# A four-block transformer stack on one core: one of its transposes per tile by VectorE and POOL, and two small products with a PSUM bank per half of the heads

## What is computed

```python
x = x + _L0_attn_ref(_layernorm(x), ...)   # linear attention, 16 heads: phi = silu + 1
x = x + _L0_ffn_ref(_layernorm(x), ...)    # silu(w1 h) * (w2 h), gelu(h1 .), gelu(h2 .), w3
x = x + _L1_attn_ref(_layernorm(x), ...)   # softmax attention over the tile's 512 tokens
x = x + _L1_ffn_ref(_layernorm(x), ...)    # tanh(h @ weight @ aux1 @ aux2 + bias)
```

## Time and profile before

| | us |
|---|---|
| median of 3 runs | 1982.96 |
| lowest and highest | 1981.56, 1984.99 |
| span of the profiled execution | 1981.5 |
| TensorE busy | 1961.9 (99%) |
| VectorE busy | 1289.0 (65%) |
| ScalarE busy | 1020.0 (51%) |
| POOL busy | 406.8 (21%) |

### The profile page before, as it was taken

How to read it: one execution, slowest core, us unless ns; L and a number is a source line. 1 busy time by engine, 2 the same in 40 slices (tenths; PEclk the granted TensorE clock), 3 DMA queues, 4 the chain that set the end, 5 groups by cost and what they waited for, 6 DMA issues and landing times.

```text
span 1981.5 us, 37810 instructions
## 1 busy us (share of the span) xinstructions
PE 1961.9 (99%) x15288; PEld 1895.6 (96%) x15288; DVE 1289.0 (65%) x3292; ACT 1020.0 (51%) x1786; POOL 406.8 (21%) x344
## 2 busy tenths in 40 slices
PE   8999999999999999999999999999999999999998
PEld 7999999999999999999999999999999999999996
DVE  6546768566685665767667676666856667676357
ACT  3445545555554655455554455555546454554433
POOL 1112212212122021311213121121220213112121
PEclk9999999999999999999999999999999999999999
DMA  9600000000000000000000000000000000000000
GB/s 359 224 3 1 22 1 12 11 2 22 1 22 1 1 22 1 22 1 1 22 1 22 1 1 22 1 22 1 23 1 1 22 1 12 1 1 12 1 1 23
DMA packets 24538, 46.03 MB, mean 23 GB/s; under 512 B 1264, under 2 KB 21488, under 8 KB 24176
## 3 DMA queue, kind: packets, MB, share of 16 engines
q1 hardware_dynamic: 24352, 43.41, 6.1%
HBM read 35.02 MB, written 19.92 MB: 28 GB/s over the span
## 4 chain that ended last, share of the span: by engine, by line
PE 97%; DMA 1%; DVE 1%; SPq 1%; issue 0%; ACT 0%; POOL 0%; DVEq 0%; ACTq 0%
PE ffn_fill L1117 49%; PE att_fill L1048 25%; PE ffn_fill L1048 13%; PE ffn_fill L1174 6%; PE att_fill L1136 1%; PE att_fill L1252 1%; DMA scratch_w2T<-in_w2T 1%; DMA w<-scratch_w1T 0%; SPq L543 0%; PE ffn_fill L1285 0%; DVE late_sm L869 0%; PE ffn_fill L1280 0%; ACT late_kv_b L1009 0%; DVE st L671 0%; DVE late_prob_t_lo L864 0%
## 5 line engine op out<-in xcount | busy, mean ns | idle before, releaser
L1117 PE MATMUL ffn_fill<-act_hi,h 128*128 128x256 f32 x4096 | 987.2, 283 | 0.8 <-issue 0.2
L1117 PE MATMUL ffn_fill<-act_lo,h 128*128 128x256 f32 x4096 | 978.2, 280 | 1.2 <-issue 1.2
L1117 PEld LDWEIGHTS ffn_fill<-act_hi,h 128*128 128x128 f32 x4096 | 770.3, 188 | 9.2 <-POOL act_lo L649 3.9
L1117 PEld LDWEIGHTS ffn_fill<-act_lo,h 128*128 128x128 f32 x4096 | 773.1, 189 | 3.6
L976 ACT ACTIVATE whole<-ffn_fill,scales 128x256 f32<-128x256 f32 x512 | 214.0, 469 | 291.3 <-PE ffn_fill L1117 290.1
L649 POOL TENSOR_TENSOR act_lo<-whole,act_hi 128x512 fp32r<-128x512 f32 x128 | 166.8, 1303 | 492.4 <-DVE act_hi L798 492.4
L802 DVE TENSOR_TENSOR act_lo<-whole,act_hi 128x512 fp32r<-128x512 f32 x256 | 183.4, 716 | 112.0 <-ACT act_hi L980 109.7
L1048 PE MATMUL ffn_fill<-half_hi,w 128*128 128x256 f32 x1024 | 245.9, 283 | 0.0
L1048 PE MATMUL ffn_fill<-half_lo,w 128*128 128x256 f32 x1024 | 244.3, 281 | 0.0
L1048 PEld LDWEIGHTS ffn_fill<-half_lo,w 128*128 128x128 f32 x1024 | 193.3, 189 | 0.1
L1048 PEld LDWEIGHTS ffn_fill<-half_hi,w 128*128 128x128 f32 x1024 | 192.5, 188 | 0.4 <-issue 0.2
(11 more groups left out here) (239 smaller groups left out, 3277.8 us busy)
## 6 DMA issues: line engine op xcount, KB each, us to landing
x<-in_L_attn_x SPq DMA_DIRECT2D x16, 512.0 KB, 3.3
out<-x SPq DMA_DIRECT2D x15, 512.0 KB, 2.9
h<-scratch_h1T SPq DMA_DIRECT2D x2, 2048.0 KB, 13.1
h<-scratch_h2T SPq DMA_DIRECT2D x2, 2048.0 KB, 13.4
w<-scratch_w1T SPq DMA_DIRECT2D x1, 1024.0 KB, 7.8
w<-scratch_w2T SPq DMA_DIRECT2D x1, 1024.0 KB, 9.8
w<-scratch_w3T SPq DMA_DIRECT2D x1, 1024.0 KB, 8.3
rows<-in_rows SPq DMA_DIRECT2D x1, 640.0 KB, 5.5
```

The source lines that it names most:

```text
L1117: last = pe.matmul(two(bank)[:, o, :], view(w), view(moving[:, k, :]), start=k == 0 and o == 0 and half == 0, stop=k == KH - 1 and half == ...
```

## The change

In the middle passes c:LT ahead of c:CF becomes c:T: the turn by VectorE into `turned`, the high part by ScalarE, the low part by POOL. On VectorE its two halves stand behind U0 and behind U1, on ScalarE and on POOL the step stands behind U1. AS and AM fill one bank for each half of the heads, which takes two banks more in place of the two that c:LT had. In the start, CHECK1 stands behind a:AQ in the list for that reason. `FIRST` and `END` keep their LT.

```diff
-    "AS": {"att_fill": 1},
-    "AM": {"att_fill": 1, "m_hi_ready": 1},
+    "AS": {"att_fill": 2},
+    "AM": {"att_fill": 2, "m_hi_ready": 2},
...
-    H0 c:CO1 c:CP2 H1 c:CO2 BST1 c:CP3 BNO1 a:AST H2 c:CO3 c:DST H3 NT1 NTL1 c:DNO W0 c:LT a:ANO U0 U1 c:CF a:T
+    H0 c:CO1 c:CP2 H1 c:CO2 BST1 c:CP3 BNO1 a:AST H2 c:CO3 c:DST H3 NT1 NTL1 c:DNO W0 c:T a:ANO U0 U1 c:CF a:T
...
@@ VectorE's order of a middle pass
-    c:LT U2 U3 a:ANO c:CF a:Ta a:Tb G0 G1 a:AKV0 a:AKV1 G2 a:AKV2 a:AKV3 a:AS G3 a:AQ a:AM a:AO n:BST0 H0
+    c:Tb U2 U3 a:ANO c:CF a:Ta a:Tb G0 G1 a:AKV0 a:AKV1 G2 a:AKV2 a:AKV3 a:AS G3 a:AQ a:AM a:AO n:BST0 H0
...
@@ TensorE
                 elif kind == "AS":
                     pe.wait_ge(s["phik_ready"], c.value("phik_ready"))
-                    bank, done = to_fill(pe, c, "att_fill", 0)
                     for g in range(KD):
+                        bank, done = to_fill(pe, c, "att_fill", g)
                         cols_g = slice(g * P, (g + 1) * P)
-                        last = product(four(bank)[:, g, :],
-                                       [(kv_b[:, b, cols_g], xn[:, b, cols_g]) for b in range(NB)])
-                    last.then_inc(done, 1)
+                        product(bank[:, 0:P], [(kv_b[:, b, cols_g], xn[:, b, cols_g]) for b in range(NB)]).then_inc(done, 1)
                 elif kind == "AM":
-                    wait_taken(pe, c, "att_fill", c.ago("att_fill", "AS", 0))
-                    bank, done = to_fill(pe, c, "att_fill", 0)
                     for g in range(KD):
-                        last = product(two(bank)[:, g, :], [(kv[:, g, :], wo[:, g, :])])
-                    last.then_inc(done, 1)
+                        wait_taken(pe, c, "att_fill", c.ago("att_fill", "AS", 0) + g)
+                        bank, done = to_fill(pe, c, "att_fill", g)
+                        product(bank[:, 0:D], [(kv[:, g, :], wo[:, g, :])]).then_inc(done, 1)
...
@@ ScalarE
                 elif kind == "AM":
-                    bank, _ = filled(act, c, "att_fill", 0)
-                    act.activation(m_sb[0], two(bank), ACT.Copy).then_inc(s["m_hi_ready"], 1)
+                    for g in range(KD):
+                        bank, _ = filled(act, c, "att_fill", g)
+                        act.activation(m_sb[0][:, g, :], bank[:, 0:D], ACT.Copy).then_inc(s["m_hi_ready"], 1)
```

More of the change, by code:

```diff
@@ L227 @@
     f:TA0 p:AO a:ANO a:LT LOOK00 LOOK01 f:TA1 m:BST0 a:AKV0 a:AKV1 f:TA2 m:BNO0 m:BT0 CHECK0
-    U0 U1 U2 U3 LOOK10 a:AB LOOK11 a:AKV2 LOOK12 a:AKV3 LOOK13 CHECK1 a:AS a:AQ
+    U0 U1 U2 U3 LOOK10 a:AB LOOK11 a:AKV2 LOOK12 a:AKV3 LOOK13 a:AS a:AQ CHECK1
     G0 a:AM G1 a:AO WIDE G2 LOOK20 LOOK21 FOLD0 TAKE0 G3 LOOK22 LOOK23 CHECK2 LOOK30
@@ L250 @@
     U0 U1 U2 U3 G0 G1a c:LT G1b c:CV c:CZ G2a c:CS0 G2b G3a c:CP0 c:CS1 c:CS2 G3b c:CO0 c:CP1 c:CS3 H0a
-    c:CO1 c:CP2 H0b c:CO2 c:CP3 H1 c:CO3 H2 H3 W0 U0 c:LT U1 U2 U3 c:CFa G0a c:CFb G0b G1 G2 G3 a:AKV0
+    c:CO1 c:CP2 H0b c:CO2 c:CP3 H1 c:CO3 H2 H3 W0 U0 U1 U2 U3 c:CFa G0a c:CFb G0b G1 G2 G3 a:AKV0
     a:AKV1 a:AKV2 a:AKV3 H0a a:AS a:AQ a:AM H0b H1a a:AO H1b H2 H3 W1"""),
@@ L267 @@
     c:CSTa U0 U1 U2 U3 c:CSTb c:CNO c:LT c:CQ c:CV c:CZ c:CS0 G0 c:CP0 c:CS1 c:CS2 c:CO0 G1 c:CP1 c:CS3 G2
-    G3 c:CO1 c:CP2 c:CO2 BST1 c:CP3 H0 BNO1 a:AST c:CO3 c:DSTa H1 c:DSTb NT1a H2 NT1b H3 NTL1 c:DNO W0 U0 U1
-    c:LT U2 U3 a:ANO c:CF a:Ta a:Tb G0 G1 a:AKV0 a:AKV1 G2 a:AKV2 a:AKV3 a:AS G3 a:AQ a:AM a:AO n:BST0 H0
+    G3 c:CO1 c:CP2 c:CO2 BST1 c:CP3 H0 BNO1 a:AST c:CO3 c:DSTa H1 c:DSTb NT1a H2 NT1b H3 NTL1 c:DNO W0 U0 c:Ta U1
+    c:Tb U2 U3 a:ANO c:CF a:Ta a:Tb G0 G1 a:AKV0 a:AKV1 G2 a:AKV2 a:AKV3 a:AS G3 a:AQ a:AM a:AO n:BST0 H0
     n:BNO0 H1 n:NT0a H2 n:NT0b H3 n:NTL0 W1"""),
@@ L284 @@
     U0 U1 U2 U3 c:LT G0 G1 c:CV c:CZ c:CS0 c:CP0 G2 c:CS1 c:CS2 c:CP1 G3 c:CS3 c:CP2 H0 c:CP3 H1 H2 H3 NT1
-    U0 U1 c:LT U2 U3 c:CF G0 a:T G1 G2 a:AKV0 a:AKV1 a:AKV2 a:AKV3 G3 a:AQ a:AM H0 H1 H2 H3 n:NT0"""),
+    U0 U1 c:T U2 U3 c:CF G0 a:T G1 G2 a:AKV0 a:AKV1 a:AKV2 a:AKV3 G3 a:AQ a:AM H0 H1 H2 H3 n:NT0"""),
     "END": order_from("""
@@ L294 @@
     "BODY": order_from("""
-    U0 U1 U2 U3 c:CST c:CB BST1 a:AST c:DST U0 U1 U2 U3 c:CF a:T a:AB n:BST0"""),
+    U0 U1 U2 U3 c:CST c:CB BST1 a:AST c:DST U0 U1 c:T U2 U3 c:CF a:T a:AB n:BST0"""),
     "END": order_from("""
@@ L834, in part @@
                         dve.wait_ge(consts, 7)
-                    bank, out = filled(dve, c, "att_fill", 0)
-                    dve.tensor_tensor(kv[:], four(bank)[:, 0:2, :], head_mask[:, None, :].broadcast_to([P, 2, P]),
-                                      ALU.mult).then_inc(out, 1)
+                    for g in range(KD):
+                        bank, out = filled(dve, c, "att_fill", g)
+                        dve.tensor_tensor(kv[:, g, :], bank[:, 0:P], head_mask[:], ALU.mult).then_inc(out, 1)
                 elif kind == "AM":
-                    bank, out = filled(dve, c, "att_fill", 0)
-                    dve.wait_ge(s["m_hi_ready"], c.value("m_hi_ready", 1))
-                    dve.tensor_tensor(m_sb[1], two(bank), m_sb[0].bitcast(F32), ALU.subtract).then_inc(out, 1)
+                    for g in range(KD):
+                        bank, out = filled(dve, c, "att_fill", g)
+                        dve.wait_ge(s["m_hi_ready"], c.value("m_hi_ready", g + 1))
+                        dve.tensor_tensor(m_sb[1][:, g, :], bank[:, 0:D], m_sb[0][:, g, :].bitcast(F32), ALU.subtract).then_inc(out, 1)
                 elif kind == "CZ":
@@ L1201, in part @@
                     pe.wait_ge(s["phik_ready"], c.value("phik_ready"))
-                    bank, done = to_fill(pe, c, "att_fill", 0)
                     for g in range(KD):
+                        bank, done = to_fill(pe, c, "att_fill", g)
                         cols_g = slice(g * P, (g + 1) * P)
-                        last = product(four(bank)[:, g, :],
-                                       [(kv_b[:, b, cols_g], xn[:, b, cols_g]) for b in range(NB)])
-                    last.then_inc(done, 1)
+                        product(bank[:, 0:P], [(kv_b[:, b, cols_g], xn[:, b, cols_g]) for b in range(NB)]).then_inc(done, 1)
                 elif kind == "AM":
-                    wait_taken(pe, c, "att_fill", c.ago("att_fill", "AS", 0))
-                    bank, done = to_fill(pe, c, "att_fill", 0)
                     for g in range(KD):
-                        last = product(two(bank)[:, g, :], [(kv[:, g, :], wo[:, g, :])])
-                    last.then_inc(done, 1)
+                        wait_taken(pe, c, "att_fill", c.ago("att_fill", "AS", 0) + g)
+                        bank, done = to_fill(pe, c, "att_fill", g)
+                        product(bank[:, 0:D], [(kv[:, g, :], wo[:, g, :])]).then_inc(done, 1)
                 elif kind == "AO":
-                    wait_taken(pe, c, "att_fill", c.ago("att_fill", "AM", 0))
+                    for g in range(KD):
+                        wait_taken(pe, c, "att_fill", c.ago("att_fill", "AM", 0) + g)
                     pe.wait_ge(s["phiq_ready"], c.value("phiq_ready"))
```

## The result

| | before | after |
|---|---|---|
| median of 4 runs | 1983.97 us | 2107.64 us |
| lowest and highest | 1981.56, 1986.16 | 2106.59, 2112.4 |
| span of the profiled execution | 1981.5 us | 2105.9 us |
| ratio, 95% interval | | 1.0634 (1.0618 to 1.0651) |

A forecast was written before the change was run, and what follows sets the result against it. TensorE, busy in 99% of the span, was taken as the bound. Per middle tile 6.8 us later plus 1.7 us of clock is 8.5, times 14 is 119 us; on 1981.5, plus 1.5, that gives 2102.0 us, range 2074 to 2130.

The forecast's parts named there:

- The relief of TensorE: Eight c:LT transposes leave TensorE in each middle tile: 0.79 us plus a 0.08 us switch, 0.87 us gained per tile.
- The turn: VectorE's 16 transposes of xn for c:T, 0.449 us each, were taken to need 7.18 us per tile.
- The stop inside U3: TensorE stands still 1.3 us in the middle of U3, until VectorE's gating products of U1 free a bank.
- The chain behind the turn: From the end of VectorE's last transpose through ScalarE's and POOL's parts to xt_lo ready: 3.28 us.
- The stop ahead of c:CF: TensorE waits for xt_lo ahead of c:CF, from 1060.1 to 1066.4: 6.3 us per tile.
- What was said to be covered: U2 and U3 for G0's last quarter, by some 2 us; AKV0, by 2.0 us; AO, by 1.0 us: no added wait.
- The clock: One fall of TensorE's clock per tile behind the 6.3 us stop, in c:CF and G0: 1.7 us lost.
- That the stops leave the clock up: Rival: the stops ahead of c:CF and inside U3 do not bring the clock down: 2078 us, chance 14%.
- That it falls twice per tile: Rival: the clock falls for longer, or once more in the 1.3 us stop: 2126 us, chance 12%.
- The third: Rival: VectorE hides the turn, c:CF does not wait and 12.2 us are gained: 1971 us, chance 4%.
- The fourth: Rival: an engine begins earlier than seen, so 0.3 to 6 us per tile are lost: 1987 to 2070 us, chance 6%.
- the price for the turn taken from the Trainium skill: VectorE's transpose at 311 ns (bf16): eight squares 2.5 us, stretch ends 4.7 us earlier, some 2012 us; not used.

The follow-up runs named there:

- e3_one_turn: Kernel after with a single c:T transpose left, behind U0, and ScalarE's and POOL's c:T behind their U0 (closing block's result not the reference's): 1973.42 us, ratio 0.9949.
- e6_turn_behind_u1: Kernel after with all 16 transposes of c:T behind U1 on VectorE, none between U0 and U1: 2111.8 us, ratio 1.0638.
- e7_cf_late: Kernel after re-ordered: c:T behind U3 on VectorE, c:CF inside G2 on TensorE, a:T and AKV to AO later: 2120.01 us, ratio 1.0684.
- e1_fill: Kernel after with 52 unused matmuls of 256 columns put into TensorE's stop ahead of c:CF: 2079.85 us, ratio 1.049.
- e2_half_turn: Kernel after with 8 of the 16 c:T transposes on VectorE left out (closing block's result not the reference's): 2059.77 us, ratio 1.0385.
- e9_gate_first: Kernel after with G0's first half ahead of c:CF on TensorE and U2's gate ahead of c:T on ScalarE: 2084.34 us, ratio 1.0512.
- e8_half_g0_first: Kernel after with the first half of G0 ahead of c:CF on TensorE instead of between its halves: 2089.58 us, ratio 1.0535.
- e5_low_by_vector: Kernel after with the two low parts of c:T subtracted by VectorE behind its turn instead of by POOL: 2090.72 us, ratio 1.0535.

## Why the prediction was right, point by point

**The relief of TensorE**: 0.87 us per tile were worked out, and the stops of the kernel after close with it to 0.02 us, as worked out under e3_one_turn. That run itself gives only 0.63 to 0.70 (9.7 us over 14), because its U's lose 0.22.

**The turn**: 16 transposes in 3.56 and 3.60 us where 7.18 was taken from a:T.

**The stop inside U3**: 1.3 us said, 1.28 between its neighbours' starts (1.40 less one step of 0.12). **The chain behind the turn**: 3.28 said, 3.23 measured (994.37 to 997.60). **The stop ahead of c:CF**: 6.3 said, 6.27 (6.39 less 0.12). From the start of W to c:CF it is 18.97 us, and 12.17 in the kernel before: **6.80 later**, as said.

**What was said to be covered**: POOL's last low part of U3 ends at 1001.00, and G0's second half, from 1004.59, never waited for it. AKV0 and AO do not stand in TensorE's list of waits for the middle tiles. Nothing was given back later either. e6_turn_behind_u1 shows that where the turn stands between U0 and U2 matters little, and e7_cf_late that there is no slack elsewhere in VectorE's chain to pay it from.

**The clock** is the term that was mis-sized: 1.7 us per tile, from two stops at the start. Worked out for each tile as the time from c:CF to AKV0 less 0.1178 us for each of its 152 matmuls, it cost 1.62 us in the first tile, 1.94 in the second, and 2.2 to 2.3 from the fifth on: 30.4 us in all, where 14 x 1.7 = 24 were said. (The same sum gives 0.03 us per tile in the kernel before.) That 1.7 came so near was in part luck: the other runs have from 1.4 to 2.9 us for stops of 4 to 5 us. e1_fill has 28.4 for the same thing by another way. The rest of the forecast then closes: 14 x 6.8 + 30.4 = 125.6 us, and 124.4 us measured between the spans; the second tile's U0 also began 0.9 us earlier than before (144.20 against 145.09), from the start phase. Where the clock fell was also put too late: the window of the stop itself averages 0.57, so it was down for most of the stop, at no cost, and stayed down through all of c:CF's first half.

**The rivals.** That the stops leave the clock up is out, by the rows at 0.50 and by e1_fill. What was said for it, a clock that is full in every slice of the page, weighed little: the page of the kernel after shows the same line. That it falls twice per tile is out for this kernel, but happened in 5 of the 14 passes of e7_cf_late. The third, that VectorE hides the turn, is out by e2_half_turn: even half of it leaves 3.9 us. Its price of 12.2 us is 2.5 more than e3_one_turn gained. The fourth, a loss between 0.3 and 6 us per tile, is out by the 6.80. Of the price for the turn taken from the Trainium skill nothing came: the 7.18 us of the row held. The 2012 us worked out with it also left the clock's term out, without a word; with 1.7 us per tile they would have been 2036. The rule behind it, to use TensorE for 128x128 where PSUM will do (the Trainium skill, VectorE: DVE Perf Modes, rules for kernel authors), is borne out here, with 7.16 us on VectorE for what took TensorE 0.79.

## What to carry to other kernels

An engine that is 65% busy has no free time where it matters if the work is put between two instructions that the bounding engine waits for: write down that stretch in the engine's own order, with durations from rows, and the wait comes out to a tenth of a microsecond. Look too for the second wait through another engine's queue, here a gate behind the copies, before moving work into a gap. And count a stop of TensorE at more than its length, since the matmuls behind it may run at the lower clock: here 1.6 to 2.3 us on top of 6.3.

## What the hardware showed that was not expected

The price of a stop to the clock does not follow its length. Stops of 4.05 us (e2_half_turn), 4.55 (e9_gate_first), 4.94 (e8_half_g0_first), 5.03 (e5_low_by_vector) and 6.27 us (after) cost 32.6, 30.1, 29.2, 30.1 and 30.4 us over their 14 tiles, and one of 8.18 us (e6_turn_behind_u1) 25.5. Nor is it the same for equal stops in one run: in e9_gate_first it alternates between 1.69 and 2.8 us from tile to tile, in e5_low_by_vector it goes up and down between 1.4 and 2.9, in the kernel after it creeps from 1.62 to 2.3 and stays. Something that does not start anew with each stop seems to be at work, but no run here was made to show what, and it stays open. In e7_cf_late the idle time ahead of c:CF is 2.3 us in all 14 passes. In nine of them the clock stayed up, as in the first row, the window of one such c:CF. In five it fell, as in the second row, where the window of the stop still had 1.00:

```profile
750.89:753.80 2.91, 2.91 (x24) 2.91 (x25) 1.71 (x4) 0.48 (x1) 0.00 (x0) 1.00 0.00 0
...
1011.85:1016.32 4.47, 4.47 (x25) 4.47 (x25) 1.72 (x4) 0.63 (x1) 0.56 (x1) 0.62 0.00 0
```

The idle time of 1.1 us inside U3 by itself was not followed by a fall: in e1_fill, which keeps it, the clock is 1.00 in all windows behind it. And 52 matmuls that nobody uses, put into the wait, made the kernel 28 us faster than the kernel after, though not than the one before.
